# Routing one row earlier and all second-half dispatches ahead of the first send, in a two-layer kernel of attention, convolution and experts

## The reference

```
xn = layernorm(x); x = x + attention(xn) + experts_top1(xn)        # layer 0
xn = layernorm(x); x = x + y_conv(xn)   + experts_top2(xn)        # layer 1

attention:    causal, one head of 128, rotated queries and keys
experts_top1: 8 experts of 128x128, capacity 512 tokens each, gate = softmax probability
y_conv:       u = xn@Wu+bu, v = xn@Wv+bv, h = 3-layer filter network of the position, decayed
              ((u * causal_fft_conv(v, h)) @ Wo + bo)
experts_top2: 8 experts, 128 -> 256 -> 128 with relu, the two best of each token, weighted
```

## Time and profile before

| | |
|---|---|
| median of 3 runs | 466.76 us (465.73 to 469.52) |
| the profiled execution, own time | 461.95 us |
| its span, first to last instruction | 460.2 us |
| mean granted TensorE clock | 0.94 of full speed |
| busy: PE, DVE, POOL, ACT | 367.6, 289.1, 241.3, 224.2 us |

### The profile page before, as it was taken

How to read it: one execution, slowest core, us unless ns; L and a number is a source line. 1 busy time by engine, 2 the same in 40 slices (tenths; PEclk the granted TensorE clock), 3 DMA queues, 4 the chain that set the end, 5 groups by cost and what they waited for, 6 DMA issues and landing times.

```text
span 460.2 us, 7726 instructions
## 1 busy us (share of the span) xinstructions
PE 367.6 (80%) x2300; PEld 296.2 (64%) x2300; DVE 289.1 (63%) x787; ACT 224.2 (49%) x551; POOL 241.3 (52%) x246
## 2 busy tenths in 40 slices
PE   0976799889999799479996989899987798788600
PEld 0751356676687558256795879899976787687500
DVE  6967375935866816853679697589549881354106
ACT  1551543351345443145252236734858789689604
POOL 5403666500663753163476666666667766666640
PEclk9998899999999979979999799999999999899955
DMA  9999921067810010010101192444422222833407
GB/s 244 350 337 189 222 69 41 30 188 195 274 42 14 25 42 19 1 35 13 37 30 40 53 269 90 116 152 149 140 86 63 69 70 65 250 97 91 121 24 255
DMA packets 60406, 52.87 MB, mean 115 GB/s; under 512 B 6442, under 2 KB 52340, under 8 KB 60110
## 3 DMA queue, kind: packets, MB, share of 16 engines
q1 hardware_dynamic: 53264, 39.10, 31.3%
q0 software_dynamic: 6656, 12.49, 8.7%
q10 hardware_dynamic: 446, 0.79, 0.6%
HBM read 30.41 MB, written 23.14 MB: 116 GB/s over the span
## 4 chain that ended last, share of the span: by engine, by line
PE 41%; DVE 22%; DMA 12%; issue 11%; ACT 6%; POOL 5%; ACTq 1%; SPq 0%; POOLq 0%; DVEq 0%
PE psS L1181 22%; PE psO L1181 11%; PE psT L1181 4%; DMA slots<-row,slot 4%; POOL slots L849 4%; DMA moe<-ys,w 2%; PE psT L1297 2%; DVE work L1878 1%; DVE work L1766 1%; DMA w<-slots 1%; ACT ring L1071 1%; ACTq L1070 1%; DMA moe<-ys,xs 1%; DVE xres L1799 1%; DMA xres<-in_x 1%
## 5 line engine op out<-in xcount | busy, mean ns | idle before, releaser
L837 POOL DMA_INDIRECT slots<-row,slot x64 | 68.7, 1074 | 35.3 <-issue 12.3
L1071 ACT ACTIVATE ring<-w 128x642 f32 x80 | 56.2, 742 | 38.5 <-DVE ys L1929 33.4
L868 POOL DMA_INDIRECT moe<-ys,xs x45 | 46.8, 1040 | 26.1 <-issue 10.1
L849 POOL DMA_INDIRECT slots<-row,slot x32 | 33.8, 1056 | 36.7 <-DVE slot L1594 18.9
L1036 ACT ACTIVATE work<-psT 128x512 f32<-128x512 f32 (+3 forms) x32 | 16.5, 517 | 68.7 <-PE psT L1297 68.7
L868 POOL DMA_INDIRECT moe<-ys,w x35 | 36.5, 1042 | 19.9 <-DMA moe<-ys,w 7.0
L1181 PE MATMUL psS<-work 128*128 128x512 f32 (+3 forms) x96 | 40.6, 534 | 6.6 <-ACT w L974 3.6
L857 POOL DMA_INDIRECT ring<-moe,slot x24 | 24.8, 1032 | 35.0 <-DMA moe<-ys 23.5
L1026 ACT ACTIVATE work<-psS,work 128x128 f32<-128x128 f32 (+7 forms) x32 | 23.6, 738 | 33.6 <-DVE work L1770 33.4
L1181 PE MATMUL psO<-work 128*128 128x128 f32 x288 | 38.9, 282 | 0.0
L1181 PEld LDWEIGHTS psO<-work 128*128 128x128 f32 x288 | 36.2, 199 | 0.0
(11 more groups left out here) (287 smaller groups left out, 861.0 us busy)
## 6 DMA issues: line engine op xcount, KB each, us to landing
slots<-xs SPq DMA_DIRECT2D x10, 516.0 KB, 12.1
mats<-in_iv SPq DMA_DIRECT2D x16, 256.0 KB, 3.8
xs<-slots SPq DMA_DIRECT2D x45, 64.5 KB, 2.0
w<-in_w SPq DMA_DIRECT2D x8, 321.0 KB, 5.2
w<-slots SPq DMA_DIRECT2D x35, 64.5 KB, 1.8
xres<-in_x SPq DMA_DIRECT2D x4, 512.0 KB, 6.1
slots<-xs SPq DMA_DIRECT2D x4, 512.0 KB, 11.2
mats<-in_fw SPq DMA_DIRECT2D x1, 2048.0 KB, 11.7
```

Source lines behind the costliest of these rows:

```text
L837: pool.indirect_dma_start(slots1[:, :], bass.IndirectOffsetOnAxis(ap=(slot1, slot2)[k][:, i:i + 1], axis=0), row[:, i, :], None, bounds_ch ...
L849: pool.indirect_dma_start(slots0[:, :], bass.IndirectOffsetOnAxis(ap=slot0[:, i:i + 1], axis=0), row[:, i, 0:D], None, bounds_check=SLOTS0 ...
L868: pool.indirect_dma_start(moe1[:, :], bass.IndirectOffsetOnAxis(ap=row_slots[m][:, D:ROWW].bitcast(I32), axis=0), ys[:, n % UNROLL, :], No ...
L1071: act.activation(pair_w[p % RING_PAIRS][:, t, :], w12[:, bass.ds(e, 1), :].rearrange("p e h -> p (e h)"), ACT.Copy).then_inc(e_w, 1)
```

## The change

Lists are moved; no computation is added or removed, but for matmuls whose result nobody reads. On the attention's rows: the additions go to earlier rows, the norms of groups 0 and 1 two rows and one row earlier, the gates of rows 21 and 22 to 19 and 21, the counts from row 24 to 23 and all routing steps one row earlier. The filter's transforms go from rows 17 and 18 to 24 and 25. The fill matmuls of rows 19, 22 and 28 are gone. On POOL: the first two norms stand two gathers earlier, the third goes from behind the last gather into the dispatches, behind the fourth, and the two halves of the last one from dispatches 6 and 14 to 12 and 21. All 32 dispatches of the second half stand ahead of the first send, where 12 did, and the rounds hold sends alone. In the prelude: gates and counts one or two projections earlier, the forward transforms in turn -1 (behind the first expert step on PE), and DVE does six radix steps before the second routing, two before its end and 14 behind it, where it did ten, twelve and none.

```diff
-FILT_RADIX_AT, FILT_RADIX_ROWS, FILT_DFT_AT = 6, 3, 17
+FILT_RADIX_AT, FILT_RADIX_ROWS, FILT_DFT_AT = 6, 3, 24
-GATES_AT = (21, 22, 29)
-NORM_AT = {20: [(0, 0), (0, 1)], 21: [(1, 0), (1, 1)], 27: [(2, 0)], 28: [(2, 1)]}
-COUNTS_AT = 24
+GATES_AT = (19, 21, 29)
+NORM_AT = {18: [(0, 0), (0, 1)], 20: [(1, 0), (1, 1)], 27: [(2, 0)], 28: [(2, 1)]}
+COUNTS_AT = 23
-WARM_PROBS = {5: 4, 7: 3, 9: 3, 19: 7, 22: 6, 26: 3, 28: 14}
+WARM_PROBS = {5: 4, 7: 3, 9: 3, 26: 3}
-ADD_BEFORE_MAX = {20: (12, 16), 25: (20, 24), 29: (24, 28), 31: (28, 30)}
-ADD_BEHIND_ROW = {16: (0, 4), 18: (4, 8), 19: (8, 12), 23: (16, 20)}
-ROUTING_BEFORE_MAX = {23: 6, 25: 8}
-ROUTING_BEHIND_ROW = {23: 6, 24: 10, 25: R1_STEPS}
+ADD_BEFORE_MAX = {29: (24, 28), 31: (28, 30)}
+ADD_BEHIND_ROW = {15: (0, 4), 16: (4, 8), 17: (8, 12), 18: (12, 16), 20: (16, 20), 25: (20, 24)}
+ROUTING_BEFORE_MAX = {22: 6, 24: 8}
+ROUTING_BEHIND_ROW = {22: 6, 23: 10, 24: R1_STEPS}
-RADIX_FIRST = 10
+RADIX_FIRST, RADIX_COUNTS = 6, 2
-SCATTER_IN_PRELUDE, SCATTER_PIECES = 12, 2
-NORM_IN_SCATTER = (6, 14)
-NORM_BEHIND_GATHER = (15, 19, 31)
+SCATTER_IN_PRELUDE, SCATTER_PIECES = 32, 2
+NORM_IN_SCATTER = (12, 21)
+NORM_BEHIND_GATHER = (13, 17)
+NORM_2_IN_SCATTER = 4
...
-        return (vu[:5] + [("t", 2 * B - 2), ("t", 2 * B - 1)] + vu[5:8] + [("g", B - 1)] + vu[8:12] + [("rc", 2)] + vu[12:]
-                + [("fw", c) for c in range(NC)])
+        return (vu[:5] + [("t", 2 * B - 2), ("t", 2 * B - 1)] + vu[5:6] + [("g", B - 1)] + vu[6:11] + [("rc", 2)] + vu[11:])
+    if r == -1:
+        return [("fw", c) for c in range(NC)]
...
+            def norms_in_scatter(j):
+                if j == NORM_2_IN_SCATTER:
+                    norm_factors(B - 2)
+                if j in NORM_IN_SCATTER:
+                    inverse_std(2 * B - 1, J // 2 * NORM_IN_SCATTER.index(j), J // 2)
             for i in range(HT):
-                if i in NORM_IN_SCATTER:
-                    inverse_std(2 * B - 1, J // 2 * NORM_IN_SCATTER.index(i), J // 2)
+                norms_in_scatter(i)
                 dispatch(0, 0, i)
...
+                    norms_in_scatter(HT + i)
                     dispatch(0, 1, i)
...
             take(passes, RADIX_FIRST)
             take(second_routing, R1_OH)
-            take(passes, RAD_F - RADIX_FIRST)
+            take(passes, RADIX_COUNTS)
             finish(second_routing)
+            take(passes, RAD_F - RADIX_FIRST - RADIX_COUNTS)
```

## The result

The changed kernel took 478.98 us, median of 4 runs (474.58 to 482.64), beside 466.25 for the kernel before (462.02 to 469.52) on the same chip: 1.027 times as long, with a 95% interval of 1.020 to 1.033. The forecast was no change, 466.4, in a range of 455.5 to 474.3; the kernel is slower and lies outside the range. Medians here are of all runs, while a ratio compares only the fast runs of either kernel, so it isn't quite the quotient of the medians. The profiled execution took 479.94 us, span 478.0, so 17.8 us of span over the one before.

The account below looks back on a forecast made before the run. The second half was taken as bound by the rounds (PE and DVE), then POOL. First send 297.9, round 4 at 311.5, round 21 at 383.3 and last sends 442.4 summed to -0.3 us: 466.4, range 455.5 to 474.3.

Parts of the forecast that it names:

- the date of the first send: On POOL, start 183.0 plus 64 dispatches, norms and row number changes: first send at 297.9, 16 us later than before.
- the end of the forward transforms: On PE behind the first expert step: they end some 3 us before their present date, so are not the bound.
- sign of being wrong: Round 4 by 305 or after 317, or rounds 4 to 13 well under 42 us without dispatches beside them.
- term "start": Earlier gates and routing in the attention put POOL's first dispatch at 183 instead of 197.53, a gain of 14.5 us.
- The half norms: On POOL among the dispatches: two half norms of tiles 24 to 31 at 1.6 us each, 3.2 us.
- port rule: DVE's radix steps would stretch the 20 moved dispatches by sharing a port pair; weighed at hundredths, so the sum stayed.
- Round 4 was predicted at 311.5: DVE's output of round 4, waiting for the first forward matrix load behind the first send: 6.6 us later than before.
- chain behind the first send: SP's queue: matrix 1 issued at 303.7 and landed at 307.0, then PE and DVE bring round 4 at 311.5.
- rival (a): POOL's list bounds throughout: last pair of sends at 423.5, 19 us early; halfway, a gain of 9 or 10; chance 0.15.
- rival (c): SP's queue behind the first send: send at 303 or later, 305.4 in its sum, 7.2 us slower; chance 0.17.
- Rival (d): Gather 19 or POOL's norm holds the routing: first dispatch at 190, first send at 305, 7 us slower; chance 0.08.
- The fill was costed at nothing: Removing PE's fill in rows 19, 22 and 28 frees time mostly in waits: zero in the sum, lower bound 3 us gain.

Follow-up runs that it names:

- e10: Kernel e6 with the last half norm behind 17 dispatches instead of 21; 457.56 us, ratio 0.985 to the kernel before.
- micro kernel: A separate kernel without the reference's computation: POOL's indirect writes beside DVE streams of one kind or none; 0.97 us per write beside no stream.
- e7: The kernel before with only the prelude's new order: radix steps 6, 2 and 14, forward transforms behind the first expert step; 484.17 us, ratio 1.043.
- e13: The kernel before with the new order of radix steps and third gates, forward transforms left where they were; 469.29 us, ratio 1.008.
- e4: The changed kernel with the forward transforms back at the end of turn -3; 476.68 us, ratio 1.027 to the kernel before.
- e3: The changed kernel with the eight forward matrices loaded behind tile 14, ahead of loads that wait for sends; 470.36 us, ratio 1.011.
- e5: The changed kernel with the fill matmuls of rows 19, 22 and 28 put back; 480.56 us, ratio 1.033 to the kernel before.
- e6: The changed kernel with 12 dispatches ahead of the first send, and radix steps and forward transforms as before; 459.82 us, ratio 0.987.
- e2: The kernel before with only all 32 dispatches of the second half ahead of the first send; 484.26 us, ratio 1.037.

## Why the prediction was wrong

**Two steps failed: the date of the first send, put at 297.9 and measured at 315.81, and the end of the forward transforms, put some 3 us earlier than before and measured 11.7 later. The first decided the time. The second was hidden behind it.** The prediction's own sign of being wrong, round 4 after 317, came true: it came at 331.42.

**The date of the first send.** The term "start" was mis-sized by 8.4 us (183 for 191.44). The gates ended at 169.0, not 164. PE's timelines show what goes into this. The profile is already 1.7 us late at row 16 (transposes at 133.53, before at 131.81), ahead of the rows that the filter's transforms left. From there to row 19 it gains only 3.4 us (144.72, before 146.36), though 7.5 us of transforms and 1.7 us of fill are gone from these rows, as PE now waits for ACT in them (1.26, 1.59 and 1.88 us). And the first gates, with their transposes and waits, now run from 145.88 to 153.11, ahead of the second; the sum had no term for these 7.2 us. From the end of the gates to the first routing step I took 6.0 us from the row of before, and it was 8.8 (177.83), as the projection between them ran at the lower clock and took 2.8 us longer. From the first step to the first dispatch it was 13.6 for 13.0. Over the profiles the first dispatch lies between 190.3 and 194.6 with the new attention and between 197.5 and 204.0 with that of before; the means of the table are 8.5 us apart, where I had 14.5. The first half was to take 62.0 us (32 dispatches, 5.9 for the third norm, 3.2 for the half norms, 2.0 for changes of row numbers) and took 69.2. The third norm was 6.75 with its wait of 3.61, close to its term; the dispatches of 4.00 and 8.30 us hold 10.4 us over their 0.97 that had no term at all, and the rest of the half took 3.2 us less than its terms. The second half was to take 52.9 and took 55.1, with 3.2 us in those of 2.10 and 3.03. 8.4 + 7.2 + 2.2 is 17.8 of the 17.9 us. No run removed the long dispatches alone, so this part is an account of one profile.

**The half norms** had a term on POOL (3.2 us) and none on the engine that waits for them. POOL's own waits for statistics went, as predicted, but DVE then waited 8.12 us for the second half norm, and in e10 an earlier place brings the experts' first output forward by 2.5 us.

**The weighing of the port rule** is where the stalls of the dispatches got lost. I let averages from the expert rounds (1.00 and 1.02 us a send) speak for stretches with another kind of DVE work beside them; there DVE's outputs and products mostly read PSUM. Beside the radix steps already had a dispatch of 1.32 us. The micro kernel separates the kinds: 0.97 us with a PSUM input, up to 1.96 with two in SBUF. The rule of the Trainium skill (SBUF - State Buffer, Who interferes with whom), which has a DVE instruction with two SBUF inputs contend with a GpSimd one that reads SBUF, agrees with that; its remark that a tensor_tensor was not seen to stall a DMA's descriptors does not.

**"The forward transforms behind the first expert step on PE end some 3 us before their present date"** was the second failed step, and it was asserted, not worked out. The 14 radix steps ended at 257.76, where the last radix step of before ended at 250.09. The transforms began at 267.35, before at 256.26, and ended at 283.17, before at 271.52. The first expert step needs expert tile 0, which is read back only after the last dispatch of the first half, and the transforms were what PE did in that wait. Moving them behind the step moved 15.6 us of matmuls (13.64 + 1.97) out of a hole and left the hole (13.21 us of idle). e7 against e13 prices it at some 16 us, alone. In the changed kernel e4 prices it at 9.1 us of round 0, since there the transforms wait 7.65 us for the radix steps even in their old place, and it is hidden by the later send, which is why the time of e4 gets nothing back.

**That the losses are alternatives, not terms,** follows. Round 4 was predicted at 311.5. With the first send at 297.9 and round 0 as it was, the send's chain gives 297.9 + 15.6 = 313.5 and round 0's 291.49 + 22.7 = 314.2. With the send as it was, the place of the transforms matters only through the two long dispatches that e4 doesn't have. So the second wrong step cost little here, and would have become the bound had the first been right.

**What held.** The chain behind the first send was right in kind: SP's first matrix load 3.9 us behind it (4 to 5 expected), a hole to round 4, and 15.6 us from send to output where the sum had 13.6; the transforms took 6.17 us for 3.72, as the granted clock was at its lower level, and that covers the 2.0. Rounds 4 to 13 took 42.9 us (42.7 predicted), 13 to 21 took 28.1 (29.1), and from round 21 to the last pair 58.2 (59.1). The pace of rounds 4 to 13 is that of before with no dispatch beside them, so it wasn't POOL's, and rival (a), POOL's list as the bound throughout, is out. e3 shows the mechanism of rival (c) by taking it away: 8.6 us come back. Its rate of one us for each us of the send was right too: it had 7.2 for a send at 305.4, which makes 17.6 for one at 315.81, and the span grew by 17.8. There is luck in how close this is: round 4 came 2.0 us later behind the send than the sum has it, and the gain behind it was 8.7 us where the sum has 6.9. The rival was the result; it had the lower chance because the start was put 8 us too early. Rival (d) had the first dispatch at 190, where it was 191.44, for another reason than it gave. The fill was costed at nothing, and e5, with it put back, is no faster.

**Shown and not shown.** Shown by a kernel of their own: the gain of the attention's lists (e6), the loss by the 32 (e2), by the place of the transforms (e7 and e13), SP's queue (e3), that the fill in its old places brings nothing (e5). For the half norm's place the profile shows it (e10) and the times don't separate it from e6. The long dispatches are a pattern in eight profiles, and the micro kernel shows it at a small size. Why the projection falls to the lower clock wasn't settled.

## What to carry to other kernels

Before moving work behind something, look at what the engine waits for there: a step that fills a wait costs little where it is and up to its full length one step later. Where two chains meet in one instruction, date both; a saving or a loss counts only from the date of the other, and a change of several parts is worth taking apart, as one part can gain while the others lose. Moving dispatches ahead of a send is free only until the send's chain becomes the later one, so look first for what another engine's queue holds behind that send. And where an engine no longer waits for another, look whether the other now waits for it.

## What the runs showed of the hardware

An indirect DMA issued by POOL takes 0.97 us, and 1.0 to 2.0 us beside DVE instructions with two SBUF inputs (0.69 us each at 512 columns, 1.2 at 1024), but 0.97 to 1.12 beside those with one SBUF input. Now and then one is held until a gapless stream of such instructions is over: 4.00, 5.88, 6.67, 7.02, 7.17, 8.11 and 8.30 us, ending 0.84 to 0.86 us after the stream in the six that were read. All eight kernels whose radix steps stand as 6, 2 and 14 show one of 6.7 to 8.3 us; with 10 and 12 the worst are 1.7 to 5.9. What decides was not tested.
